# First attention: its last four heads as straight code without look-ahead, the last sum's store and the x load in other places

## The chip, the cores and the metric

One core of a Trainium2 chip runs the whole program in one launch. The metric is the device time in microseconds of that launch, median of several runs. The engines named below are TensorE (PE), VectorE (DVE), ScalarE (ACT), GpSimd (POOL) and SyncE (SP), whose instruction stream issues nearly all DMAs.

## The reference, cut to what matters

```python
x = x + L0_xattn(layernorm(x), ctx_512, ...)   # latent cross attention, 8 batches x 16 heads
x = x + L0_ffn(layernorm(x), ...)              # feed-forward on 64 chosen rows of each sequence
x = x + L1_xattn(layernorm(x), ctx_512, ...)
x = x + L1_ffn(layernorm(x), ...)              # mixture of experts
```

In the first attention, for each of 8 batches and 16 heads: queries of 256 positions are projected to 192 numbers (`q_big`), turned by their rotary table, projected into the 64-number space of the context rows; scores against 1601 context rows, softmax, and a weighted sum of the rows (`ctx_c`, 256 x 64). An output projection follows:

```python
scores = einsum('bhsr,bhlr->bhsl', q_r, k_r)
attn = softmax(scores)
ctx_c = einsum('bhsl,bld->bhsd', attn, kv_r)
ctx = einsum('bhsd,hkd->bhsk', ctx_c, w_kc_kv) ... ; return ctx @ Wo.T
```

## The kernel before, in words

The program is a row of stages, each a block in which every engine has its own instruction stream; at the end of a block all engines meet. The change lies at the end of `phase_attention0` and at the start of `phase_project0_ffn0`, which follows it.

**The attention stage** works on `N` = 128 heads (8 batches x 16). Head n is pipelined over the engines, with orders written out by hand. The main part is a loop of 32 turns on each of PE, ACT, DVE and POOL, four heads (`AHEAD`) a turn; the body is the same for every head apart from odd and even ones. For head n, PE's body (L927 and on) runs:

- `scores` (L826): the rest of the scores of head n and most of those of head n+1. 26 matmuls of 256 columns a head, in four groups g of key tiles (4, 4, 4 and 1 tiles). 22 of the 26 in a body belong to head n+1.
- `values` (L844, L847): the weighted sum of head n, 26 pairs of matmuls, 129 and 65 columns, one with the probabilities' high parts (`prob`), one with their low parts (`rest`). They add into the PSUM tile `c_psV`.
- `maxima` (L810): eight matmuls of 400 or 401 columns for head n+2, whose row maxima DVE takes (`reduce_max`, L1132) and joins (`join`).
- `shift` (L814): one transposition of these maxima for head n+1.
- the queries of later heads, made for a pair p of heads at a time: `q_first` (L764, 12 matmuls) in odd bodies and `q_second` (L764, 6) in even ones, `q_lat_high` (L790, 6) and `q_lat_low` (L796, 3) in odd ones, all of 256 columns. DVE, ACT and POOL turn and split them (`turn_first`, `turn_second`, `rope_high`, `rope_low` L1251, `q_high`, `q_low`).

ACT takes the exponential of each score group (`exp`, L1011) and, when all of head n's values are summed, drains `c_psV` (L1077). POOL makes the low parts (`rest_of`, L1243: three large ones and a small one per head; it takes the probabilities minus their rounded high part), and in `total` (L1257, L1259) adds the two halves of the drained tile of head n-1 and keeps the softmax sum in `rec`. A `rest_of` of group g waits for that group's exponential; `values` of group g wait for that `rest_of`; the exponential of group g of the next head waits for those `values`, as there is one buffer per group.

So the look-ahead of the last turn belongs to heads 128 and 129, which don't exist: the loop computes them from the first batch's data, which SP loads once more for it (`batch_steps(B - 1, 0)`, with `last=following` the refills of keys and values).

SP stores each head's sum to DRAM (`acc_scr`, L715), the last after the loops (L744), and then waits until everything it issued has landed. DVE, after its loop, inverts the first batch's sums of softmax and scales that batch's rows (`scale_heads`, L518, two multiplications of 1024 columns). The end of the block follows.

**The next stage** projects and normalizes batch by batch. For batch b, DVE scales the rows of batch b+1 (`scale_batch`, L518), adds the projection to x (`add_rows`, L1507), takes statistics, logits and the choice of rows; PE transposes the scaled rows (`turn`, L1624) and projects them (`project`, L1633). PE's projection of batch b+1 waits until the addition of batch b has emptied its PSUM tile. Before the first scaling DVE waits for five small constant loads, and before the first addition for the whole of x:

```python
            sp.dma_start(x[:], t["x"]...).then_inc(in_x, 16)          # L1454, 2 MB
            ... five small loads: br, wr, upper, iota, base           # L1455 to L1459
            for b in range(2, B):
                sp.wait_ge(t_full, 4 * (b - 2) + 4)
                load_heads(sp, t, keep, b)                            # L511, 2 x 512 KB
            ...
            dve.wait_ge(in_c, 80)                                     # the five
            for b in range(B):
                if b + 1 < B:
                    scale_batch(dve, nc.vector, b + 1)
                add_rows(b)                                           # b == 0: waits in_x
```

Of the kernel before, what the change touches and what calls it, by code (L numbers as in the profile page):

```python
# [522 lines left out]
def phase_attention0(nc, ctx, t, keep):  # L523
# [102 lines left out]
    with nc.Block() as block:  # L626
        @block.sync
        def _(sp):
# [94 lines left out]
            def batch_steps(b, following):  # L723
# [18 lines left out]
            batch_steps(B - 1, 0)  # L742
            sp.wait_ge(summed, 2 * N + 2)
            sp.dma_start(t["acc_scr"][N], acc[1][:, :, DC:2 * DC]).then_inc(sent[1], 16)  # L744
            for u in range(2):
                sp.wait_ge(sent[u], 16 + 16 * (N // 2))
            sp.wait_ge(in_wA, 16 * (N // 2 + 4))
            sp.wait_ge(in_wR, 16 * (N // 2 + 3))
            for g in range(4):
                sp.wait_ge(in_kk[g], 32 * (B + 1))  # L750
                sp.wait_ge(in_v[g], 16 * (B + 1))
            for c in range(len(CHUNKS)):
                sp.wait_ge(in_kkm[c], 16 * (B + 1))
            sp.wait_ge(in_xb, 32 * (B + 1))
            sp.wait_ge(in_m, 16 * (N // 2 + 3))

        @block.tensor
        def _(pe):
# [168 lines left out]
            with pe.Fori(0, N // AHEAD) as j:  # L927
                for u in range(AHEAD):
# [41 lines left out]
                    maxima(n + 2, p2, 7, s2)  # L970

        @block.scalar
        def _(act):
# [29 lines left out]
            def exp(n, g, slot):  # L1003
                lo, hi = GROUPS[g]
                r = P if hi < LT else LLAST
                w = (hi - lo) * S
                act.wait_ge(s_full, 4 * n + g + 1)

                act.wait_ge(in_kk[(g + 2) % 4], 32 * ((n + (g + 2) // 4) // H0) + 32)
# [47 lines left out]
            with act.Fori(0, N // AHEAD) as j:  # L1057
                for u in range(AHEAD):
# [20 lines left out]
                    if u % 2 == 0:  # L1079
                        rope_high(p, slice(2, 3), ropedR)  # L1080

        @block.vector
        def _(dve):
# [42 lines left out]
            def reduce_max(n, k):  # L1126
                c, st = divmod(k, ST)
                dve.wait_ge(mx_full, PASSES * n + k + 1)
                if st == 0:
# [72 lines left out]
            with dve.Fori(0, N // AHEAD) as j:  # L1202
                for u in range(AHEAD):
# [22 lines left out]
                    reduce_max(n + 2, 7)  # L1226
            dve.wait_ge(summed, 2 * H0 + 2)
# [3 lines left out]
            dve.wait_ge(keep["in_acc"][0], 32)  # L1231
            for s in range(ST):
                scale_heads(nc.vector, keep, 0, s)

        @block.gpsimd
        def _(pool):
# [17 lines left out]
            def total(n, i):  # L1254

                pool.wait_ge(pv_drained, n + 1)
                nc.gpsimd.tensor_tensor(acc[i][:, :, DC:2 * DC], acc[i][:, :, DC:2 * DC], acc[i][:, :, 0:DC],  # L1257
                                        ALU.add).then_inc(summed, 1)
# [15 lines left out]
            with pool.Fori(0, N // AHEAD) as j:  # L1274
# [11 lines left out]
            total(N, 1)  # L1286
# [102 lines left out]
def phase_project0_ffn0(nc, ctx, t, keep, ahead, x, xn):  # L1389
# [1446 lines left out]
def build(nc, t):  # L2836
    LIVE.clear()
    with ExitStack() as whole:
        def sb(ctx, name, shape, dt=F32):
# [21 lines left out]
            "rec": rec,  # L2861
            "in_acc": [new_semaphore(nc, f"in_acc{i}") for i in range(2)],
# [109 lines left out]
```

## Time and profile before

| | us |
|---|---|
| median of 3 runs | 1640.25 (1639.94 to 1640.4) |
| the profiled execution's own time | 1644.53 |
| its span, first to last instruction | 1642.9 |
| PE busy in the span | 1567.9 |
| DVE busy | 1308.3 |
| POOL busy | 1153.0 |
| ACT busy | 1062.5 |

The loop of the attention stage ends near 1145 us of the span; the next stage's first instructions stand at 1148.3 us. The span is read stage by stage: in each, the engine that is never idle, or the wait that ends last, sets the length. In a timeline a row's first number is its start from the span's beginning, the second its length; matmuls are pipelined, so two that follow each other without a gap are told apart by their starts. The brackets give the idle time before a row and what ended it.

### The profile page before, as it was taken

How to read it: one execution, taken by the hardware profiler on the slowest of the kernel's cores; microseconds unless marked ns; L12 is line 12 of the kernel's file. 1: busy time of each engine (PE TensorE's matmuls, PEld its weight loads, DVE VectorE, ACT ScalarE, POOL GpSimd, SP SyncE). 2: the span in 40 equal slices, each digit the busy share in tenths (PEclk: the TensorE clock that was granted, in tenths of full speed). 3: DMA queues.
4: the chain of work that ended last, by engine and by line, in shares of the span. 5: the costliest groups of instructions: out<-in, count | busy, mean ns of one | idle time of the engine just before them, and what ended most of it. 6: DMA issues, size and time to landing. Idle time of an engine off the chain costs nothing. (4 is left out here: it accounts for less than half of the span.)

```text
span 1642.9 us, 50082 instructions
## 1 busy us (share of the span) xinstructions
PE 1567.9 (95%) x16337; PEld 1280.1 (78%) x16337; DVE 1308.3 (80%) x3062; ACT 1062.5 (65%) x2174; POOL 1153.0 (70%) x1102
## 2 busy tenths in 40 slices
PE   5879999999999999999999999999999899999998
PEld 4658888888888888888888888887886445556787
DVE  6888888888898888888898888888783578885223
ACT  5877777777777777777777777776322466664121
POOL 5439999999999999999999999998100214431321
PEclk8699999999999999999999999999999999999999
DMA  9731121121122122112112115312840011101344
GB/s 259 237 89 49 48 81 49 49 76 49 48 64 65 40 66 72 42 57 74 48 46 83 40 56 127 76 54 76 212 86 1 15 35 65 66 8 54 101 149 161
DMA packets 184952, 126.23 MB, mean 77 GB/s; under 512 B 107578, under 2 KB 172008, under 8 KB 184512
## 3 DMA queue, kind: packets, MB, share of 16 engines
q1 hardware_dynamic: 183360, 121.53, 26.4%
q0 software_dynamic: 1536, 3.99, 0.7%
q8 instruction: 31, 0.51, 0.1%
q14 instruction: 25, 0.20, 0.0%
HBM read 82.24 MB, written 24.48 MB: 65 GB/s over the span
## 5 line engine op out<-in xcount | busy, mean ns | idle before, releaser
L1243 POOL TENSOR_TENSOR c_rest<-c_prob 128x1024 f16<-128x1024 f32 (+1 forms) x513 | 817.1, 1608 | 37.8 <-ACT c_prob L1011 16.7
L1132 DVE TENSOR_REDUCE c_mxp<-c_psM 128x1 f32<-128x400 f32 (+1 forms) x1040 | 578.1, 571 | 56.8 <-PE c_psM L810 37.1
L1011 ACT ACTIVATE c_prob<-c_psS,ln,c_exp_scale 128x1024 f32<-128x1024 f32 (+1 forms) x514 | 528.3, 1040 | 145.1 <-PE c_psS L826 141.8
L826 PE MATMUL c_psS<-c_q,c_kk 128*128 128x256 f16 (+1 forms) x3350 | 513.0, 273 | 0.5 <-DVE c_ropeA L1091 0.4
L844 PE MATMUL c_psV<-c_vb,c_prob 128*128 128x129 f16 (+1 forms) x3328 | 420.5, 221 | 1.1 <-ACT c_acc L1077 1.1
L847 PE MATMUL c_psV<-c_vb,c_rest 128*128 128x65 f16 (+1 forms) x3328 | 394.5, 193 | 0.0
L826 PEld LDWEIGHTS c_psS<-c_q,c_kk 128*128 128x128 f16 (+1 forms) x3350 | 311.0, 99 | 66.2 <-issue 1.0
L810 PE MATMUL c_psM<-c_kkm,c_q 128*128 128x400 f16 (+1 forms) x1040 | 347.0, 334 | 3.5 <-DVE c_mxp L1132 2.9
L847 PEld LDWEIGHTS c_psV<-c_vb,c_rest 128*128 128x128 f16 (+1 forms) x3328 | 303.0, 98 | 28.7
L844 PEld LDWEIGHTS c_psV<-c_vb,c_prob 128*128 128x128 bf16 (+1 forms) x3328 | 312.7, 98 | 14.0 <-ACT c_acc L1077 1.4
L2221 ACT ACTIVATE g_prob<-g_psS,g_bias 128x128 f32<-128x128 f32 (+1 forms) x256 | 103.8, 426 | 49.8 <-DVE g_bias L2271 49.8
L1251 POOL TENSOR_TENSOR c_ropedL<-c_roped,c_ropedH 128x512 f16<-128x512 f32 (+1 forms) x132 | 118.4, 915 | 21.7 <-ACT c_ropedH L979 14.7
L810 PEld LDWEIGHTS c_psM<-c_kkm,c_q 128*128 128x128 f16 x1040 | 101.1, 97 | 10.0 <-DVE c_mxp L1132 4.2
L979 ACT ACTIVATE c_ropedH<-c_roped 128x512 f16<-128x512 f32 (+1 forms) x132 | 68.9, 522 | 48.5 <-DVE c_roped L1097 48.2
L764 PE MATMUL c_psS<-c_xb,c_w2s 128*128 128x256 f16 x768 | 94.3, 273 | 0.0
L1323 POOL TENSOR_SCALAR xn_rows<-x_rows,f_n_agg,f_n_rstd 128x256 f32<-128x256 f32 x3 | 3.9, 1316 | 128.5 <-DVEq L1340 128.5
L2676 DVE TENSOR_TENSOR m_g<-m_s,m_psH 128x256 f32<-128x256 f32 (+1 forms) x48 | 20.0, 419 | 78.6 <-ACT m_s L2623 66.8
L764 PEld LDWEIGHTS c_psS<-c_xb,c_w2s 128*128 128x128 f16 x768 | 73.3, 98 | 9.8
L986 ACT ACTIVATE c_q<-c_psQ 64x256 f16<-64x256 f32 x132 | 49.8, 377 | 47.5 <-PE c_psQ L796 46.0
L999 ACT ACTIVATE c_q<-c_psM 32x128 f16<-32x128 f16 x258 | 68.8, 267 | 9.4 <-PE c_psM L814 3.2
L1087 DVE TENSOR_TENSOR c_ropeB<-c_psS,c_tabB 128x256 f32<-128x256 f32 x128 | 48.4, 420 | 33.2 <-PE c_psS L764 33.2
L2623 ACT ACTIVATE m_s<-m_psH 128x256 f32<-128x256 f32 (+1 forms) x48 | 18.2, 382 | 80.8 <-PE m_psH L2500 69.6
(336 smaller groups left out, 2491.3 us busy)
## 6 DMA issues: line engine op xcount, KB each, us to landing
c_w2s<-w_scr SPq DMA_DIRECT2D x67, 256.0 KB, 2.6
c_ms<-m_scr SPq DMA_DIRECT2D x67, 192.0 KB, 2.7
c_w2s<-w_scr SPq DMA_DIRECT2D x66, 128.0 KB, 2.0
acc_scr<-c_acc SPq DMA_DIRECT2D x129, 64.0 KB, 2.0
kv<-acc_scr SPq DMA_DIRECT2D x16, 512.0 KB, 6.3
m_w<-in_L_ffn_W SPq DMA_DIRECT2D x16, 352.0 KB, 3.5
c_vb<-V SPq DMA_DIRECT2D x27, 129.0 KB, 2.0
c_kk<-KK SPq DMA_DIRECT2D x27, 128.0 KB, 2.0
```

What stands on the lines that cost most here:

```text
L764: mm = pe.matmul(out, weights[:, w, c], xb[:, x, c, :], start=(c == 0 and i == 0), stop=(c == DK - 1 and i == 2))
L810: pe.matmul(psM[:, st, 0:w], q1[slot][:, st * P:(st + 1) * P], kkm[:, c0:c0 + w], start=True, stop=True).then_inc(mx_full, 1)
L826: mm = pe.matmul(psS[g % 2][0:r, i * S:(i + 1) * S], src[:, (lo + i) * P:(lo + i) * P + r], mov[slot][:, :], start=(one == 0 and i % 2 == ...
L844: pe.matmul(psV[:, st * W:(st + 1) * W], high[0:r, c0:c0 + P], vb[0:r, i, :], start=(i == 0 and st == 0), stop=False, skip_group_check=True)
L847: mm = pe.matmul(psV[:, st * W + DC:(st + 1) * W], rest[g][0:r, c0:c0 + P], vb[0:r, i, DC:W], start=False, stop=(i == LT - 1), skip_group_ ...
L979: nc.scalar.activation(ropedH[:, blocks, :], roped[:, blocks, :], ACT.Copy).then_inc(rh_done, 1)
L999: last = nc.scalar.activation(q2[slot][0:2 * SHIFT_ROWS, st * P:(st + 1) * P], shiftT[st * 2 * SHIFT_ROWS:(st + 1) * 2 * SHIFT_ROWS, :], A ...
L1011: nc.scalar.activation(prob[g][0:r, 0:w], psS[g % 2][0:r, 0:w], ACT.Exp, bias=keep["ln1024"][0:r, :], scale=exp_scale[slot][0:r, :]).then_ ...
L1132: nc.vector.tensor_reduce(mxp[:, st, c:c + 1], psM[:, st, 0:CHUNKS[c][1]], AX.X, ALU.max).then_inc(mx_done, 1)
L1243: nc.gpsimd.tensor_tensor(rest[g][0:r, 0:w], prob[g][0:r, 0:w], high[0:r, 0:w], ALU.subtract).then_inc(rest_done, 1)
L1251: nc.gpsimd.tensor_tensor(ropedL[:, blocks, :], roped[:, blocks, :], ropedH[:, blocks, :], ALU.subtract).then_inc(rl_done, 1)
L2221: ins = nc.scalar.activation(prob[k % 2][:, i * w:(i + 1) * w], psS[k % 2][:, i * w:(i + 1) * w], ACT.Exp, bias=bias[k % 2][:, i:i + 1], a ...
```

## The change

PE, ACT, DVE and POOL run 31 turns of their loops instead of 32, and the last four heads (124 to 127) are written out after them. In that code:

- PE has no query matmuls (`q_first`, `q_second`, `q_lat_high`, `q_lat_low`), no scores and no transposition for head 128, no maxima for heads 128 and 129. The order of the rest is as before but for small moves; where the maxima of a further head stood ahead of scores, head 126's body waits for ACT's `shift_copy` itself.
- ACT has no `rope_high`, `q_high`, `q_other`, and no exponentials for head 128.
- DVE has no turns and `q_low`, and no maxima beyond head 127. After its loop it inverts the first batch's sums as before, and then waits for POOL's last low part (`rest_done` of 4 N) before it scales.
- POOL has no `rope_low` and no low part of head 128. The last `total` writes to a place inside the large tile `kv` (`last_acc`) that outlives the stage.
- SP has no query loads and no refills for these four heads; it stores the sums of heads 123 to 126, and not the last one.

The next stage's SP stream begins with the store of that last sum, then the five small constant loads, then x; the load of batch 7's heads, which reads that sum, waits for the store.

```diff
-                four(H0 // AHEAD - 1, last=following)
+                if not ends:
+                    four(H0 // AHEAD - 1, last=following)
...
-            batch_steps(B - 1, 0)
-            sp.wait_ge(summed, 2 * N + 2)
-            sp.dma_start(t["acc_scr"][N], acc[1][:, :, DC:2 * DC]).then_inc(sent[1], 16)
+            batch_steps(B - 1, 0, ends=True)
+            for n in range(N - AHEAD, N):
+                sp.wait_ge(summed, 2 * n + 2)
+                sp.dma_start(t["acc_scr"][n], acc[(n + 1) % 2][:, :, DC:2 * DC]).then_inc(sent[(n + 1) % 2], 16)
...
-            with pe.Fori(0, N // AHEAD) as j:
+            with pe.Fori(0, N // AHEAD - 1) as j:
...
+            for u in range(AHEAD):
+                n, s1, s2 = N - AHEAD + u, (u + 1) % AHEAD, (u + 2) % AHEAD
+                scores(n, 2, u, (6, 8))
+                scores(n, 3, u)
+                values(n, 0, (0, 1))
+                if n + 2 < N:
+                    maxima(n + 2, (n + 2) // 2, 0, s2)
+                values(n, 0, (1, 4))
+                if n + 1 < N:
+                    scores(n + 1, 0, s1, (0, 4))
+                    pe.wait_ge(mcol_done, 2 * n + 4)
+                    shift(n + 1)
+                values(n, 1, (0, 2))
+                if n + 2 < N:
+                    maxima(n + 2, (n + 2) // 2, 1, s2)
+                elif n + 1 < N:
+                    pe.wait_ge(shift_done, n + 2)
...
+                values(n, 3)
+                if n + 1 < N:
+                    scores(n + 1, 2, s1, (0, 6))
+                if n + 2 < N:
+                    maxima(n + 2, (n + 2) // 2, 7, s2)
...
+            for u in range(AHEAD):
+                n = N - AHEAD + u
+                exp(n, 2, u)
+                if n + 1 < N and u % 2 == 0:
+                    shift_copy(n + 1, (u + 1) % AHEAD)
+                exp(n, 3, u)
+                if n + 1 < N and u % 2 == 1:
+                    shift_copy(n + 1, (u + 1) % AHEAD)
+                if n + 1 < N:
+                    exp(n + 1, 0, (u + 1) % AHEAD)
+                    exp(n + 1, 1, (u + 1) % AHEAD)
+                act.wait_ge(pv_done, 4 * n + 8)
...
+            for u in range(AHEAD - 1):
+                n = N - AHEAD + u
+                join(n + 1)
+                if n + 2 < N:
+                    for k in range(PASSES):
+                        if k == PASSES - 1:
+                            scale_of(n + 2, (u + 2) % AHEAD)
+                        reduce_max(n + 2, k)
             dve.wait_ge(summed, 2 * H0 + 2)
...
             dve.wait_ge(keep["in_acc"][0], 32)
+            dve.wait_ge(rest_done, 4 * N)
             for s in range(ST):
                 scale_heads(nc.vector, keep, 0, s)
...
-            total(N, 1)
+            for n in range(N - AHEAD, N):
+                rest_of(n, 1)
+                rest_of(n, 2)
+                rest_of(n, 3)
+                total(n, (n + 1) % 2)
+                if n + 1 < N:
+                    rest_of(n + 1, 0)
+            total(N, 1, keep["last_acc"])
...
-            sp.dma_start(x[:], t["x"].rearrange("b (s p) d -> p (b s) d", p=P)).then_inc(in_x, 16)
+            sp.dma_start(t["acc_scr"][B * H0], keep["last_acc"]).then_inc(keep["last_sent"], 16)
             sp.dma_start(br[:], t["L0_ffn_b_r"].partition_broadcast(P)).then_inc(in_c, 16)
...
             sp.dma_start(base[:], t["cap_base"]).then_inc(in_c, 16)
+            sp.dma_start(x[:], t["x"].rearrange("b (s p) d -> p (b s) d", p=P)).then_inc(in_x, 16)
             for b in range(2, B):
                 sp.wait_ge(t_full, 4 * (b - 2) + 4)
+                if b == B - 1:
+                    sp.wait_ge(keep["last_sent"], 16)
                 load_heads(sp, t, keep, b)
```

## Rows read from the trace of the kernel before

**Rows 1.** The span, from the view of cores.

```profile
core 0: 1642.9 us, clock 0.980
```

**Rows 2.** Windows: length, PE, PE load, DVE, ACT, POOL, clock, DMA share.

```profile
1113.20:1129.30 16.10, 16.10 (x204) 13.94 (x201) 14.32 (x35) 12.20 (x21) 15.74 (x15) 1.00 0.22 64
1145.90:1162.00 16.10, 11.77 (x57) 10.11 (x58) 6.66 (x10) 3.16 (x6) 7.82 (x2) 0.89 0.82 217
1280.00:1300.00 20.00, 17.29 (x92) 9.63 (x89) 12.42 (x38) 13.45 (x26) 8.34 (x6) 1.00 0.00 0
```

**Rows 3.** Timeline of POOL at the end of the attention: start, us, line, operation.

```profile
1112.41 4.42 POOL L1243 TENSOR_TENSOR c_rest<-c_prob 128x1024 f16<-128x1024 f32 x3 [0.21 <-ACT c_prob L1011]
...
1117.50 2.25 POOL L1243 TENSOR_TENSOR c_rest<-c_prob 128x1024 f16<-128x1024 f32 x1
1119.72 1.78 POOL L1251 TENSOR_TENSOR c_ropedL<-c_roped,c_ropedH 128x512 f16<-128x512 f32 x2
...
1137.50 4.31 POOL L1243 TENSOR_TENSOR c_rest<-c_prob 128x1024 f16<-128x1024 f32 x3
...
1144.68 0.45 POOL L1257 TENSOR_TENSOR c_acc<-c_acc 128x128 f32<-128x128 f32 x1 [0.22 <-ACT c_acc L1077]
```

**Rows 4.** Timeline of PE there: start, us (pipelined), line, count.

```profile
1143.42 0.33 PE L810 MATMUL c_psM<-c_kkm,c_q 128*128 128x401 f16 x1
1143.59 0.22 PE L844 MATMUL c_psV<-c_vb,c_prob 65*128 65x129 f16 x1
...
1143.68 0.22 PE L844 MATMUL c_psV<-c_vb,c_prob 65*128 65x129 f16 x1
...
1143.77 0.82 PE L826 MATMUL c_psS<-c_q,c_kk 128*128 128x256 f16 x6
1144.42 0.33 PE L810 MATMUL c_psM<-c_kkm,c_q 128*128 128x401 f16 x1
1148.49 0.30 PE L1624 MATMUL e_ps<-kv 128*128 128x128 f32 x1 [3.74 <-PEq L626]
```

**Rows 5.** Timeline of ACT there, the last drain.

```profile
1144.22 0.38 ACT L1077 ACTIVATE c_acc<-c_psV 128x258 f32<-128x258 f32 x1
```

**Rows 6.** Timeline of DVE: one turn addition, then the stage boundary.

```profile
1117.32 0.68 DVE L1097 TENSOR_TENSOR c_roped<-c_ropeA,c_ropeB 128x512 f32<-128x512 f32 x1
...
1145.66 2.36 DVE L518 TENSOR_TENSOR kv<-kv 128x1024 f32<-128x1024 f32 x2
...
1159.43 2.36 DVE L518 TENSOR_TENSOR kv<-kv 128x1024 f32<-128x1024 f32 x2 [9.09 <-DMA e_base<-in_cap_base]
1161.71 0.74 DVE L1507 TENSOR_TENSOR x_rows<-x_rows,e_ps 128x256 f32<-128x256 f32 x2
...
1168.24 1.23 DVE L518 TENSOR_TENSOR kv<-kv 128x1024 f32<-128x1024 f32 x1
```

**Rows 7.** Timeline of the DMA queue of SP (its issues) at the boundary.

```profile
1145.45 0.60 SPq L744 DMA_DIRECT2D acc_scr<-c_acc  x1
1148.31 0.39 SPq L1454 DMA_DIRECT2D x_rows<-in_x  x1
...
1152.12 0.47 SPq L1459 DMA_DIRECT2D e_base<-in_cap_base  x1
1152.65 5.94 SPq L511 DMA_DIRECT2D kv<-acc_scr  x2
```

**Rows 8.** DMA issues of the boundary: count, KB, us from issue to landing.

```profile
x_rows<-in_x SPq DMA_DIRECT2D x1, 2048.0 KB, 9.7
...
e_upper<-in_upper SPq DMA_DIRECT2D x1, 32.0 KB, 6.0
...
e_base<-in_cap_base SPq DMA_DIRECT2D x1, 8.0 KB, 7.1
...
kv<-acc_scr SPq DMA_DIRECT2D x1, 512.0 KB, 8.2
...
acc_scr<-c_acc SPq DMA_DIRECT2D x3, 64.0 KB, 2.0
```

More of the change, by code:

```diff
@@ L721, in step, with batch_steps @@
                     refill_values(sp, last, 3)
-            def batch_steps(b, following):
+            def batch_steps(b, following, ends=False):
                 def four(j, last=None, x=None):
@@ L970, in _ @@
                     maxima(n + 2, p2, 7, s2)
+            for u in range(AHEAD):
[16 more added lines that the diff above has]
+                if n + 1 < N:
+                    scores(n + 1, 0, s1, (4, 8))
+                if n + 2 < N:
+                    maxima(n + 2, (n + 2) // 2, 2, s2)
+                values(n, 1, (2, 4))
+                if n + 2 < N:
+                    maxima(n + 2, (n + 2) // 2, 3, s2)
+                if n + 1 < N:
+                    scores(n + 1, 1, s1, (0, 2))
+                values(n, 2, (0, 1))
+                if n + 2 < N:
+                    maxima(n + 2, (n + 2) // 2, 4, s2)
+                if n + 1 < N:
+                    scores(n + 1, 1, s1, (2, 6))
+                if n + 2 < N:
+                    maxima(n + 2, (n + 2) // 2, 5, s2)
+                if n + 1 < N:
+                    scores(n + 1, 1, s1, (6, 8))
+                values(n, 2, (1, 4))
+                if n + 2 < N:
+                    maxima(n + 2, (n + 2) // 2, 6, s2)
+                values(n, 3)
+                if n + 1 < N:
+                    scores(n + 1, 2, s1, (0, 6))
+                if n + 2 < N:
+                    maxima(n + 2, (n + 2) // 2, 7, s2)
         @block.scalar
@@ L1007, in exp @@
                 act.wait_ge(s_full, 4 * n + g + 1)
-                act.wait_ge(in_kk[(g + 2) % 4], 32 * ((n + (g + 2) // 4) // H0) + 32)
+                if not (isinstance(n, int) and n + (g + 2) // 4 == N):
+                    act.wait_ge(in_kk[(g + 2) % 4], 32 * ((n + (g + 2) // 4) // H0) + 32)
                 act.wait_ge(pv_done, 4 * n + g + 1)
@@ L1056, in _ @@
             q_other(1, 2)
-            with act.Fori(0, N // AHEAD) as j:
+            with act.Fori(0, N // AHEAD - 1) as j:
                 for u in range(AHEAD):
@@ L1128, in reduce_max @@
                 dve.wait_ge(mx_full, PASSES * n + k + 1)
-                if st == 0:
+                if st == 0 and not (isinstance(n, int) and n + (c + 1) // len(CHUNKS) == N):
                     dve.wait_ge(in_kkm[(c + 1) % len(CHUNKS)],
@@ L1201, in _ @@
             q_low(1, 2)
-            with dve.Fori(0, N // AHEAD) as j:
+            with dve.Fori(0, N // AHEAD - 1) as j:
                 for u in range(AHEAD):
@@ L1252, in rope_low, with total @@
                                         ALU.subtract).then_inc(rl_done, 1)
-            def total(n, i):
+            def total(n, i, out=None):
                 pool.wait_ge(pv_drained, n + 1)
-                nc.gpsimd.tensor_tensor(acc[i][:, :, DC:2 * DC], acc[i][:, :, DC:2 * DC], acc[i][:, :, 0:DC],
-                                        ALU.add).then_inc(summed, 1)
+                nc.gpsimd.tensor_tensor(acc[i][:, :, DC:2 * DC] if out is None else out, acc[i][:, :, DC:2 * DC],
+                                        acc[i][:, :, 0:DC], ALU.add).then_inc(summed, 1)
                 nc.gpsimd.tensor_copy(keep["rec"][:, bass.ds(n, 1), :].rearrange("p o s -> p (o s)"),
@@ L1273, in _ @@
             pool.wait_ge(v_low, B)
-            with pool.Fori(0, N // AHEAD) as j:
+            with pool.Fori(0, N // AHEAD - 1) as j:
                 for u in range(AHEAD):
@@ L2861, in build @@
             "rec": rec,
+            "last_acc": kv[:, B * LT * DC - n_rec + ST - ST * DC:B * LT * DC - n_rec + ST].rearrange(
+                "p (s d) -> p s d", s=ST),
+            "last_sent": new_semaphore(nc, "last_sent"),
             "in_acc": [new_semaphore(nc, f"in_acc{i}") for i in range(2)],
```

19 lines of the change are left out of this document (10 added, 9 removed).

## The prediction

> **What bounds the kernel now.** First the cores: one core, a span of 1642.9 us [rows 1]. The profiled execution took 1644.53 us, the median of the runs is 1640.25; I take the sum against the span of 1642.9 and carry the difference over to the median unchanged. The change touches only the last four heads of the first attention and the entry of the next stage, so everything before about 1112.4 us of the span, and everything after about 1168 us, should keep its length and only move. The windows say who is full: in a pair of heads, 16.10 us, PE is busy for all 16.10, POOL for 15.74 and DVE for 14.32 [rows 2]. PE sets the pace and POOL stands 0.4 us behind it. So work taken from PE alone is worth little; what is taken from POOL counts. The timelines of POOL, PE, ACT and DVE then show the end: POOL finishes the low parts of head 127 at 1137.50 + 4.31 = 1141.81 [rows 3]; PE still has work up to 1144.4, and the drain waits for it at 1144.22 [rows 4, 5]; the next stage issues its first DMA at 1148.31 [rows 7]. There DVE stands still for 9.09 us until the constant `e_base` lands [rows 6].
>
> **1. What PE loses.** In-order starts give a price each: six score matmuls from 1143.77 to 1144.42, 0.109 us each; a maxima matmul 0.17 (1143.42 to 1143.59); a values pair 0.09 (1143.59 to 1143.68) [rows 4]. Removed are 24 + 12 + 18 query matmuls and 22 scores, 76 x 0.109 = 8.3 us, and 16 maxima, 2.7 us, together 11.0 (the one transposition is below 0.1). Four heads, two windows of 16.1 less a little, take 32.1 us of PE; 21.0 or so remain [rows 2].
>
> **2. What the four heads then cost: POOL.** POOL begins head 124's low parts at 1112.41 and ends head 127's at 1141.81, 29.40 us. Of that only the two pairs of `rope_low`, 1.78 us each, are useless: 3.56 [rows 3]. 25.84 us remain, above PE's 21.0, so POOL becomes the bound and the last low part ends at 1138.25. The removed low part of head 128 came after it and belongs to step 3. From below: beside DVE's turn addition of 0.68 us the low part takes 2.25 us, 0.36 more than the 1.89 that it takes otherwise (4.42 for two large and a small one leaves about that) [rows 3, 6]; with the turns gone two such excesses go, 0.7 us at most. From above: POOL waited 0.21 us for an exponential before head 124 [rows 3]; if it does so two times a head now that nothing separates its parts, that is 4 x 0.4 = 1.6 us less the 0.7 that is idle already (twice 16.10 - 15.74 [rows 2]), 0.9. I take 0, between the two.
>
> **3. From the last low part to the next stage.** Now 6.50 us pass from 1141.81 to 1148.31: head 128's low part, the total at 1144.68, the store of 0.60 us at 1145.45 that lands 2.0 us later, and DVE's scaling, 1145.66 + 2.36 = 1148.02, which ends last; 0.29 us more to the first issue [rows 3, 6 to 8]. Afterwards DVE waits for the last low part, scales in 2.36, and the stage ends 0.29 later: 2.65. Beside it lie two to eight values pairs of head 127 (0.7 us at 0.09 [rows 4]), the drain of 0.38 [rows 5] and the total of 0.45 and its small copy, 1.8 us in all with the handovers: hidden under the scaling by 0.6. But that total runs beside a DVE multiplication that reads two tensors of SBUF, and the low part above paid 0.36 for such a neighbour [rows 3, 6]. Cost 0 if hidden, 0.65 if the total can only start when the scaling is over; I take 0.25, nearer to the row. The inversion of the sums (DVE has been idle) and the store cost nothing here; with cover gone they would be 0.34 and 2.0. So 6.50 becomes 2.90: 3.60 gained. The Trainium skill (SBUF — State Buffer, Terms, "shared port pair") says that the loser of that port fully blocks and doesn't share bandwidth; by it the 0.65 would be paid and the sum be 0.4 worse. The low part's excess of 0.36 beside 0.68 neither proves nor denies it, as their starts differ (1117.50 against 1117.32).
>
> The stage's end thus moves from 1148.31 to 1141.15, by 3.56 + 3.60 = 7.16 us.
>
> **4. The entry of the next stage.** Call its start S. Now `add_rows(0)` starts at S + 13.40 (1161.71): the constants land at 1152.12 + 7.1 = S + 10.9, and the scaling of batch 1, 2.36 us, comes after them; x has landed at S + 9.7 and is not waited for [rows 6 to 8]. Afterwards SP issues the store (0.60 where x took 0.39) and the constants, the last at S + 4.0. With no 2 MB in front they land in about the 2.0 us of a store [rows 8], S + 6, and batch 1 is scaled by S + 8.5 while PE is busy with batch 0. x is issued at S + 4.34 + 0.21 = S + 4.55 [rows 7]. Its landing took 9.7 us with 232 KB of constants among its 2048; scaled by 2048/2280 it is 8.7. I take the middle, 9.2: x lands at S + 13.75 and the addition starts at S + 13.85, 0.45 later than now. Bounds: 8.7 us gives S + 13.35, nothing; the case with batch 2's loads between is a rival. So the 9.09 us stall isn't gained: the wait for constants is replaced by one for x, since x now starts 4.2 us later. The Trainium skill (DMA: Bandwidth & Descriptors, Queues, rings and completion order) has each DMA engine take descriptors in ring order; by it loads issued behind x can't hold it up, and x would land with the 32 KB load behind it, `e_upper`, at 1151.16 + 6.0 or 8.9 us after its issue, 0.3 better than my sum. The row has it at 9.7, later than that small load, so the order of landings isn't that of the issues [rows 8].
>
> Batch 2's rows: their first load landed at 1152.65 + 8.2, 7.4 us before DVE scales them at 1168.24; the second was held in the queue until 1158.59, 9.6 us before [rows 6 to 8]. All that traffic now starts 4.2 us after S later, so some 3 us of slack stay: 0. The removed refills and query loads had nobody behind them but the end: 0. The new wait on `last_sent` stands before batch 7's load, six batches after a store of 2 us: 0.
>
> **Sum:** -3.56 - 3.60 + 0.45 = -6.7 us; span 1636.2, median 1640.25 - 6.7 = 1633.5 us.
>
> **The rivals.** (a) x comes later still: batch 2's two loads of 512 KB are issued right behind it (now 4.3 us after it [rows 7]) and share the engines with it. If one of them gets ahead it costs 9.2 x 512/2048 = 2.3 us, both 4.6: 1635.8 to 1638.1 us. For it speaks that landings overtake each other; against it that x moved ahead of everything now. (b) The four heads don't shorten: PE waits for low parts, ACT for PE, POOL for exponentials in a ring, and step 2 gives nothing: 1637.0. For it: single buffers per group, so each part hands over to the next; against: PE has 4.8 us to spare over four heads. (c) Slower: PE has gaps in the four heads, 21.0 of 25.84 us busy, 81%, and the granted clock falls to its lower level (1.2 instead of 2.4 GHz). If it fell for all of it, PE would need 42.0 us, 16.2 more than POOL: 1649.7. It decides once 4.8 us of its work run at half, and the result is slower than before when 11.5 us do. Against it: at 17.29 of 20.00 us busy the clock was 1.00; for it: around PE's idle 3.74 us the mean was 0.89 [rows 2, 4]. (d) The change doesn't do what it says, as something else holds the stage's end: that would be seen as (b) with step 3 gone too, 1640.7.
>
> **How the numbers follow.** The forecast 0.62, with its own range 1631.1 (rests shorter by 0.7, no port cost, x 0.45 earlier, the idle 0.7 gone, and the 0.3 by which runs differ: 2.4 in all) to 1635.8; (a) 0.18; (b) 0.13; (c) 0.04; (d) 0.03. The range is 1631.1 to 1638.1, to the end of (a); (c) and (d) stay out. 0.2%, about what a measurement of this kernel can tell from no change, is 3.3 us: faster means under 1637.0. That takes in the forecast, two thirds of (a) and half of (b): 0.81; within 0.2%: 0.15; slower: 0.04.
>
> **What would show it.** In the changed profile: POOL's last L1243 ends about 25.8 us after head 124's first one (rival b: 29.4), PE has gaps before `values` and POOL none; DVE's L518 follows within 0.1 us; the first SP issue of the next stage comes 2.9 us after the last low part; DVE's stall in front of L1507 names x_rows, with L518 of batch 1 near S + 6; from there to the end the distances are those of before. The prediction is wrong if L1507 starts before S + 12.5 or after S + 15, if the clock leaves 1.00 within the four heads, or if a stage after 1168 us changes its length by over 1 us.

## The result, and the profile after

The changed kernel takes 1630.49 us (median of 4 runs, 1630.03 to 1631.92); the kernel before, run beside it, 1640.1 us (1638.79 to 1640.4). The ratio is 0.9944, with a 95% interval of 0.9933 to 0.9956: about 9 us faster, where 6.7 were forecast. 1630.5 lies 0.6 us below the low end of the range. The profiled execution took 1630.33 us.

The span, from the view of cores:

```profile
core 0: 1628.5 us, clock 0.983
```

POOL's timeline of the last four heads (the page's columns: start, us, line, operation, idle time before it and what ended it), to be laid beside [rows 3]:

```profile
1109.44 6.37 POOL L1308 TENSOR_TENSOR c_rest<-c_prob 128x1024 f16<-128x1024 f32 x4
...
1116.69 1.89 POOL L1308 TENSOR_TENSOR c_rest<-c_prob 128x1024 f16<-128x1024 f32 x1 [0.34 <-ACT c_prob L1052]
1118.77 4.38 POOL L1308 TENSOR_TENSOR c_rest<-c_prob 128x1024 f16<-128x1024 f32 x3 [0.18 <-ACT c_prob L1052]
...
1124.07 1.89 POOL L1308 TENSOR_TENSOR c_rest<-c_prob 128x1024 f16<-128x1024 f32 x1 [0.38 <-ACT c_prob L1052]
...
1131.29 6.17 POOL L1308 TENSOR_TENSOR c_rest<-c_prob 128x1024 f16<-128x1024 f32 x4 [0.17 <-ACT c_prob L1052]
1137.41 0.46 POOL L1322 TENSOR_TENSOR c_acc<-c_acc 128x128 f32<-128x128 f32 x1
1137.81 1.18 POOL L1324 COPY kv<-c_acc 128x2 f32<-128x2 f32 x1
1138.95 0.45 POOL L1322 TENSOR_TENSOR kv<-c_acc 128x128 f32<-128x128 f32 x1
1139.35 1.18 POOL L1324 COPY kv<-c_acc 128x2 f32<-128x2 f32 x1
```

Head 124's first low part starts at 1109.44 and head 127's last ends at 1131.29 + 6.17 = 1137.46: 28.02 us. Before, it was 31.50: the 29.40 us of the prediction begin at 1112.41, with head 124's second low part, and the first, which stands 2.10 us ahead of it at 1110.31, belongs to the stretch:

```profile
1110.31 1.89 POOL L1243 TENSOR_TENSOR c_rest<-c_prob 128x1024 f16<-128x1024 f32 x1
```

POOL's waits for an exponential are short, 0.17 to 0.38 us, and there are five of them.

The same stretch as a window (length, PE, PE load, DVE, ACT, POOL, clock, DMA share, GB/s):

```profile
1109.44:1137.46 28.02, 24.33 (x331) 20.61 (x329) 13.21 (x33) 18.63 (x27) 26.63 (x23) 1.00 0.05 11
```

POOL is busy for 26.63 of 28.02 us, PE for 24.33, and the granted clock is 1.00, the upper of its two levels. In the kernel before, the same stretch has POOL busy for 30.60 of 31.50 us and PE for all 31.50:

```profile
1110.31:1141.81 31.50, 31.50 (x399) 27.38 (x396) 28.02 (x68) 23.83 (x40) 30.60 (x27) 1.00 0.27 82
```

DVE at the boundary, beside [rows 6]:

```profile
1137.59 2.90 DVE L518 TENSOR_TENSOR kv<-kv 128x1024 f32<-128x1024 f32 x2 [9.53 <-POOL c_rest L1308]
...
1146.21 2.36 DVE L518 TENSOR_TENSOR kv<-kv 128x1024 f32<-128x1024 f32 x2 [2.79 <-DMA e_base<-in_cap_base]
1153.65 0.75 DVE L1582 TENSOR_TENSOR x_rows<-x_rows,e_ps 128x256 f32<-128x256 f32 x2 [5.08 <-DMA x_rows<-in_x]
...
1159.71 1.23 DVE L518 TENSOR_TENSOR kv<-kv 128x1024 f32<-128x1024 f32 x1
```

The scaling of the first batch follows the last low part by 0.13 us, takes 2.90 instead of 2.36, and has ended by 1140.49, but the next stage starts only at 1141.39. What it starts on is in SP's queue (beside [rows 7]) and in the waits of SP (line waited for: total, times, longest):

```profile
1139.02 0.53 SPq L746 DMA_DIRECT2D acc_scr<-c_acc  x1
1141.39 0.34 SPq L1526 DMA_DIRECT2D acc_scr<-kv  x1
1141.78 0.43 SPq L1527 DMA_DIRECT2D e_br<-in_L_ffn_b_r  x1
...
1143.68 0.43 SPq L1531 DMA_DIRECT2D e_base<-in_cap_base  x1
1144.15 0.43 SPq L1532 DMA_DIRECT2D x_rows<-in_x  x1
1144.98 8.32 SPq L511 DMA_DIRECT2D kv<-acc_scr  x2
```

```profile
SPq L626 <- DMA acc_scr<-c_acc: 1.2, 1, 1.2
```

The store of head 126's sum is issued at 1139.02, when POOL's copy (1137.81 + 1.18) is through, and SP waits at the end of the block until it has landed. Call the first issue of the next stage S again (1141.39). The x load is issued at S + 2.76 and lands 9.5 us later (beside [rows 8]):

```profile
x_rows<-in_x SPq DMA_DIRECT2D x1, 2048.0 KB, 9.5
```

### The profile page after: what moved, and what is told of

Its sections match the earlier page's. It is cut to its first block and busy times, and to the rows that moved or that the text cites. A ratio compares the mean times of both kernels' runs of the same rounds, so it can differ in the third digit from the quotient of the medians.

```text
span 1628.5 us, 49586 instructions
## 1 busy us (share of the span) xinstructions
PE 1555.9 (96%) x16244; PEld 1269.8 (78%) x16244; DVE 1291.7 (79%) x3021; ACT 1055.8 (65%) x2158; POOL 1150.2 (71%) x1097
## 5 line engine op out<-in xcount | busy, mean ns | idle before, releaser
L1188 DVE TENSOR_REDUCE c_mxp<-c_psM 128x1 f32<-128x400 f32 (+1 forms) x1024 | 569.5, 572 | 59.4 <-PE c_psM L807 40.2
L807 PE MATMUL c_psM<-c_kkm,c_q 128*128 128x400 f16 (+1 forms) x1024 | 341.7, 334 | 4.1 <-DVE c_mxp L1188 2.9
L1316 POOL TENSOR_TENSOR c_ropedL<-c_roped,c_ropedH 128x512 f16<-128x512 f32 (+1 forms) x128 | 114.8, 916 | 21.7 <-ACT c_ropedH L1019 14.7
L2353 DVE COPY g_pT<-g_psT 128x1024 f32<-128x1024 f32 x48 | 58.7, 1224 | 14.0 <-PE g_psT L2199 12.9
```

What stands on the lines that cost most here:

```text
L807: pe.matmul(psM[:, st, 0:w], q1[slot][:, st * P:(st + 1) * P], kkm[:, c0:c0 + w], start=True, stop=True).then_inc(mx_full, 1)
L1188: nc.vector.tensor_reduce(mxp[:, st, c:c + 1], psM[:, st, 0:CHUNKS[c][1]], AX.X, ALU.max).then_inc(mx_done, 1)
L1316: nc.gpsimd.tensor_tensor(ropedL[:, blocks, :], roped[:, blocks, :], ropedH[:, blocks, :], ALU.subtract).then_inc(rl_done, 1)
```

## The experiments

Twelve kernels were run, in three groups, each group on one chip with the kernel before beside it (medians of before: 1646.21, 1639.67 and 1647.54 us). Between chips only ratios are compared. One table holds the steps, all read from timelines as above. R3 is the end of the last low part; "chain" is the time from head 124's first low part to the scaling of batch 2 in the next stage, the first point after which every kernel does the same at the same distances, up to the entry of the second attention (below). In the kernels whose next stage doesn't begin with the store (before, before_again, x_moved_alone, last_store_in_stage), S is its first issue all the same. Every experiment has one trace, the kernels before and after have two each; between the two of one kernel, the chain differs by 0.25 to 0.28 us.

| kernel | start to R3 | R3 to S | S to `add_rows(0)` | S to batch 2 | chain | ratio of the run, 95% interval |
|---|---|---|---|---|---|---|
| before | 31.50 | 6.50 | 13.40 | 19.93 | 57.93 | |
| before_again | 31.50 | 6.50 | 13.68 | 20.21 | 58.21 | 0.9999 (0.9989 to 1.0008) |
| after | 28.02 | 3.93 | 12.26 | 18.32 | 50.27 | 0.9944 (0.9933 to 0.9956) |
| after_again | 28.00 | 3.94 | 12.03 | 18.08 | 50.02 | 0.9944 (0.993 to 0.9958) |
| x_first | 28.02 | 3.93 | 13.15 | 19.68 | 51.63 | 0.9955 (0.9942 to 0.9969) |
| x_moved_alone | 31.5 | 6.49 | 11.77 | 18.02 | 56.0 | 0.9988 (0.9979 to 0.9997) |
| no_low_wait | 29.71 | 2.94 | 11.95 | 18.01 | 50.66 | 0.9944 (0.9931 to 0.9958) |
| early_total_half_scale | 28.56 | 2.13 | 12.17 | 18.23 | 48.92 | 0.9943 (0.9929 to 0.9956) |
| last_store_in_stage | 28.0 | 5.52 | 11.49 | 18.82 | 52.35 | 0.9957 (0.9945 to 0.9969) |
| last_head_low_on_dve | 26.52 | 3.07 | 12.45 | 18.51 | 48.10 | 0.9931 (0.9917 to 0.9945) |
| all_together | 26.51 | 2.08 | 12.24 | 18.29 | 46.88 | 0.9934 (0.992 to 0.9948) |
| pe_keeps_useless | 30.61 | 3.93 | 12.04 | 18.56 | 53.10 | 0.9962 (0.9947 to 0.9977) |
| x_split | 28.01 | 3.93 | 7.40 | 18.01 | 49.95 | 0.995 (0.9938 to 0.9963) |
| low_on_dve_x_split | 26.52 | 3.07 | 8.63 | 19.28 | 48.87 | 0.9939 (0.9927 to 0.9951) |

**Where x is loaded.** The theory of the prediction says that x's later issue costs 0.45 us; the result says that it is a gain. Two kernels ask this from both sides. x_first is the changed kernel with x ahead of the constants; x_moved_alone is the kernel before with x behind them and nothing else changed.

```diff
+            sp.dma_start(x[:], t["x"]...).then_inc(in_x, 16)
             sp.dma_start(br[:], ...)
...
-            sp.dma_start(x[:], t["x"]...).then_inc(in_x, 16)
```

> The changed kernel with one edit undone: in the next stage's SP stream x (2 MB) is loaded ahead of the five constants again, behind the last sum's store. Theory (the constants' issues and landings are slow behind x): the DVE stall in front of the scaling of batch 1 is back, near 9 us, that scaling starts about 11 us after the stage's first issue S instead of 4.8, the first addition at S + 13.4 instead of S + 12.3, and PE's spread of batch 0 follows later, so 1.1 to 1.6 us more than the changed kernel's 1630.5: 1631.6 to 1632.1. Rival (x's landing alone decides, as the prediction had it, 0.45 in favour of x first): 1630.0.

> The kernel before with one part of the change alone: x is loaded behind the five constants; tail and store as before. Theory: the same 1.1 to 1.6 us as between the changed kernel and x_first, so about 1638.7 against 1640.1. The prediction's own step 4: 0.45 slower, 1640.5. If the last sum's store ahead of the constants is what matters: no change.

SP's queue in x_first and then in x_moved_alone:

```profile
1143.37 0.43 SPq L1527 DMA_DIRECT2D x_rows<-in_x  x1
1143.85 2.10 SPq L1528 DMA_DIRECT2D e_br<-in_L_ffn_b_r  x1
1145.98 0.43 SPq L1529 DMA_DIRECT2D e_wr<-in_L_ffn_W_r  x1
```

```profile
1148.65 0.34 SPq L1454 DMA_DIRECT2D e_br<-in_L_ffn_b_r  x1
1149.04 0.43 SPq L1455 DMA_DIRECT2D e_wr<-in_L_ffn_W_r  x1
...
1150.95 0.42 SPq L1459 DMA_DIRECT2D x_rows<-in_x  x1
```

Behind the 2 MB load one constant's issue takes 2.10 us (in before_again two take 1.28 and 1.16), ahead of it 0.34 to 0.43. So x ahead costs SP 1.5 to 1.7 us of issuing, and the constants are slow to land; x behind waits for 2.3 us of issues only. The move gives the kernel before 1.9 to 2.2 us on the chain (ratio 0.9988, 2.0 us, by its interval 0.5 to 3.5), and undoing it takes 1.4 to 1.6 from the changed kernel (by the ratios, 0.9955 against 0.9944, it can't be told from nothing), whose DVE row then reads:

```profile
1153.86 2.36 DVE L518 TENSOR_TENSOR kv<-kv 128x1024 f32<-128x1024 f32 x2 [8.84 <-DMA e_base<-in_cap_base]
```

The old stall of about 9 us is back. A rival for a part of the loss is the clock: from S to batch 2's scaling its mean is 0.84 in x_first, with PE busy for 19.29 of 19.68 us, and 0.91 in the changed kernel, with 17.75 of 18.32. But `add_rows(0)` follows DVE's scaling without a gap in x_first, and at that point 0.9 to 1.1 of the 1.4 to 1.6 us are there already. Only the rest, behind it, can be the clock's.

**Is x then the next thing to shorten?** x_split loads batch 0's part of x ahead of the constants and the rest behind them.

```diff
+            sp.dma_start(x[:, 0:ST], t["x"][0:1]...).then_inc(in_x, 16)
             sp.dma_start(br[:], ...)
...
-            sp.dma_start(x[:], t["x"]...).then_inc(in_x, 16)
+            sp.dma_start(x[:, ST:NT], t["x"][1:B]...).then_inc(in_xr, 16)
```

> The changed kernel with the load of x in two: batch 0's 256 KB behind the last sum's store and ahead of the constants, the other seven batches where x is now. Theory: DVE's wait of 5 us for x goes, but PE is busy with batch 0's projections and batch 1's transpositions until S + 12.4 and spreads batch 0's logits only after the projection that follows, so the third scaling comes 0.3 to 0.5 us earlier: 0.4 us faster, and the wait moves from x to PE. Rival (x's wait is worth its length): 2 us or more faster.

```profile
1149.29 0.41 DVE L1585 TENSOR_TENSOR x_rows<-x_rows,e_ps 128x256 f32<-128x256 f32 x1
1152.63 0.42 DVE L1585 TENSOR_TENSOR x_rows<-x_rows,e_ps 128x256 f32<-128x256 f32 x1 [2.93 <-PE e_ps L1711]
```

The first addition comes 4.9 us earlier, at S + 7.40, without a wait for x; its second half then waits for PE, and batch 2's scaling starts only 0.3 us earlier than in the changed kernel (0.1 against after_again). The wait for x of 5.08 us in DVE's rows is hidden but for that, and the ratios agree (0.995 against 0.9944). What it hid behind is PE, which in the 12 us behind S is busy for 11.81 at a clock of 0.86 in the changed kernel already. The same 12 us in the two kernels with x split, first x_split, then low_on_dve_x_split:

```profile
1141.89:1153.89 12.00, 11.81 (x62) 10.91 (x63) 5.92 (x14) 3.57 (x6) 7.82 (x2) 0.86 0.82 233
```

```profile
1141.93:1153.93 12.00, 11.72 (x50) 10.56 (x51) 4.75 (x8) 2.75 (x4) 7.81 (x2) 0.75 0.86 236
```

PE is full in both, at a mean granted clock of 0.86 and 0.75, and where it is 0.75 batch 2's scaling comes at S + 19.28 instead of 18.01.

**What holds the end of the attention.** The prediction put DVE's scaling last. The rival is SP's wait for the store of head 126's sum. early_total_half_scale makes POOL take that total ahead of head 127's low parts, and leaves half of the scaling to the next stage; last_store_in_stage puts the last sum's store back into the attention; no_low_wait drops DVE's wait for the last low part.

```diff
+                if n == N - 1:
+                    total(n, (n + 1) % 2)
                 rest_of(n, 1)
...
-            for s in range(ST):
-                scale_heads(nc.vector, keep, 0, s)
+            scale_heads(nc.vector, keep, 0, 0)
...
+            scale_heads(nc.vector, keep, 0, 1)
```

> The changed kernel with two moves at its end: POOL's total of head 126 comes ahead of head 127's second low part instead of behind its last one, and DVE scales only the first half of batch 0 before the stage's end and the second half first thing in the next stage. Theory (the store of head 126's sum, issued 1.6 us after the last low part and landed 2.0 us later, ends the stage): the last low part 0.6 later, but only the last total (1.85 us) and 0.3 behind it, so the next stage starts 2.5 to 2.8 us after the last low part instead of 3.9: 0.6 to 0.8 us faster, 1629.8, and SP waits for no landing at the end. Rival (the end is held by DVE's scaling or by a fixed barrier of 0.9 us behind it): the gap between the last work and the first issue stays 0.9.

```diff
+            sp.wait_ge(summed, 2 * N + 2)
+            sp.dma_start(t["acc_scr"][N], acc[1][:, :, DC:2 * DC]).then_inc(sent[1], 16)
...
-            total(N, 1, keep["last_acc"])
+            total(N, 1)
...
-            sp.dma_start(t["acc_scr"][B * H0], keep["last_acc"])...
```

> The changed kernel with one part undone: the last head's sum is stored by the attention stage again, after its total, and SP waits for it there; the next stage's stream begins with the constants. Theory: the last total ends 3.1 us after the last low part (its copy held by DVE's scaling), the store lands 2.0 us later and the next stage starts 0.37 after that, 5.4 us after the last low part instead of 3.9; SP then reaches x 0.4 earlier. Net 1.1 us slower than the changed kernel. Rival (the store was hidden under something else): no change, as with the prediction's step 3, which put DVE's scaling at the end.

```diff
-            dve.wait_ge(rest_done, 4 * N)
```

> The changed kernel without DVE's wait for the last low part: DVE scales the first batch as soon as its own work is done, about 9 us earlier, beside POOL's low parts. The result is the same. Theory of an exclusive port: each of the two multiplications holds POOL for up to 1.2 us, the last low part comes up to 2.4 us later, and the end after it shrinks from 3.9 to about 3.0 us, since the copy of 1.18 us is 0.18 again and the store follows earlier: net 1 to 1.5 us slower, 1631.5 to 1632. Rival, the port is shared at half the cost: 0.3 slower, 1630.8. Rival, no contention: the end alone shrinks, 1629.6.

POOL at the end of no_low_wait and, below, its DVE row:

```profile
1128.39 5.36 POOL L1307 TENSOR_TENSOR c_rest<-c_prob 128x1024 f16<-128x1024 f32 x3 [0.19 <-ACT c_prob L1052]
1133.72 1.43 POOL L1321 TENSOR_TENSOR c_acc<-c_acc 128x128 f32<-128x128 f32 x1
...
1141.36 0.45 POOL L1321 TENSOR_TENSOR c_acc<-c_acc 128x128 f32<-128x128 f32 x1
1141.76 0.18 POOL L1323 COPY kv<-c_acc 128x2 f32<-128x2 f32 x1
```

```profile
1130.33 4.50 DVE L518 TENSOR_TENSOR kv<-kv 128x1024 f32<-128x1024 f32 x2
```

In no_low_wait the scaling is over long before the end, and the stage still ends 2.94 us after R3: total 0.40 to its successor, copy 0.18, store 2.0, and some 0.4 to the first issue. In the changed kernel the copy takes 1.18, and 3.93 us pass: 0.99 more, the copy's excess of 1.00. With the store of head 126 out of the way (early_total_half_scale, whose last total follows the drain at R3 + 1.04), 2.13 us are left: the last copy, again of 0.18 us, ends 0.34 us before S, and head 126's store has landed some 4 us before S. (This kernel moves the total and half of the scaling at once, and which of the two gives how much isn't shown.) With the last store back in the stage it is 5.52, the store's issue at 1142.69 following a second copy of 1.18; so moving that store is worth 1.6 us at the end. On the chain it is 2.1, where 1.1 were expected; the other 0.5 lie behind S, where the clock's mean is 0.86 instead of 0.91 and PE is busy for 18.58 of 18.82 us, and it isn't shown that the store's place brings them. The chain of the end is thus total, copy, store, landing in the changed kernel, in no_low_wait and in last_store_in_stage (there with the last head's store), and DVE's scaling decides through the 1.00 us by which it delays the copy.

no_low_wait also prices the wait itself: started early, the scaling runs beside low parts, three of which take 5.36 instead of 4.42 us and a total 1.43 instead of 0.46. Start to R3 grows by 1.7 us, the end shrinks by 1.0, and the chain is 0.4 to 0.6 longer than in the changed kernel, where 1 to 1.5 were expected. The ratios, 0.9944 both, can't tell that apart. DVE pays as much as POOL here: its two multiplications take 4.50 us instead of 2.36, the second alone 2.95.

**What bounds the four heads.** pe_keeps_useless adds 48 matmuls of 256 columns on PE's last four bodies, twelve in each, some 5.2 us, that nobody reads. last_head_low_on_dve gives head 127's low parts to DVE.

```diff
                 scores(n, 3, u)
...
+                q_rows(psQ[:, 0:S], wR)
+                q_rows(psQ[:, 0:S], wR)
```

> The changed kernel with useless work put back on PE alone: 12 query matmuls of 256 columns in each of the last four bodies, 48 x 0.109 = 5.2 us, into a PSUM tile that nobody reads. Theory (POOL bounds the written-out heads): PE goes from 21.0 to 26.2 us in 28.0, so most of it fits its gaps: head 124's first low part to the last one from 28.0 to at most 29.2 us. Rival (the ring through PE, ACT and POOL bounds them, each handover in series): all 5.2 us are added, 33.2 us.

```diff
             for n in range(N - AHEAD, N):
-                rest_of(n, 1)
-                rest_of(n, 2)
-                rest_of(n, 3)
+                if n < N - 1:
+                    rest_of(n, 1)
+                    rest_of(n, 2)
+                    rest_of(n, 3)
...
+            for g in range(len(GROUPS)):
+                nc.vector.tensor_tensor(rest[g]..., prob[g]..., high..., ALU.subtract).then_inc(rest_done, 1)
             dve.wait_ge(rest_done, 4 * N)
```

> The changed kernel with head 127's four low parts made by DVE, which stands idle there, instead of POOL. Theory (POOL's low parts bound the written-out heads): they end 1.3 to 1.8 us earlier, as DVE takes about 1.2 us for a large one where POOL takes 1.9 and the exponentials are there early; the last low part then follows the last exponential by about 1.5 us. End and entry as in the changed kernel: 1.3 to 1.8 us faster. Rival (the ring through PE and ACT bounds them): the last low part stays where it is, no change.

The added 5.2 us of PE cost 2.6 (28.0 to 30.61), and POOL's longest wait for an exponential grew from 0.4 to 1.3 us. Neither theory had that. PE was idle for 3.7 us (24.33 of 28.02 busy), so at least 1.5 of the 5.2 had no room, and PE is now busy for 28.77 of 30.61 us, POOL for 26.59. That the other 1.1 us are lost because every low part, exponential and `values` hands over to the next in one buffer is argued and not shown. Taking four of POOL's sixteen low parts away gives 1.5 us of the 6.2 that they take, as DVE then does them in 4.2:

```profile
1132.90 2.49 DVE L1303 TENSOR_TENSOR c_rest<-c_prob 128x1024 f16<-128x1024 f32 x2 [3.38 <-ACT c_prob L1052]
1135.74 1.68 DVE L1303 TENSOR_TENSOR c_rest<-c_prob 128x1024 f16<-128x1024 f32 x2 [0.35 <-ACT c_prob L1052]
1137.45 2.66 DVE L518 TENSOR_TENSOR kv<-kv 128x1024 f32<-128x1024 f32 x2
```

Its end is shorter too, 3.07 instead of 3.93: POOL, freed of head 127's low parts, takes head 126's total at 1134.42, and the store behind it, issued at 1135.86, lands 3.0 us later, 1.6 us before S. That is one more sign that this store held the end.

**All at once, and both kernels again.** all_together is last_head_low_on_dve with half of the scaling moved to the next stage; low_on_dve_x_split joins last_head_low_on_dve to x_split; before_again and after_again are the two kernels unchanged.

> The low parts of head 127 on DVE, POOL's total of head 126 as early as it can be, and the second half of batch 0 scaled in the next stage. Theory: both gains add, since one shortens the heads and the other the end behind them: head 124's first low part to the third scaling of the next stage 47.3 to 47.8 us where the changed kernel has 50.3, early_total_half_scale 48.9, so 2.5 to 3 us faster than the changed kernel. Rival: with the low parts gone from POOL the exponentials bound head 127, and the second gain is only half there: 1.5 us.

> Two gains in one kernel: head 127's low parts on DVE (1.9 us between head 124's first low part and the third scaling of the next stage in its own trace) and x in two loads (0.4 expected): 47.7 us for that distance where the changed kernel has 50.0 to 50.3. If the clock at the entry of the second attention stays at its upper level, the median is 2.3 us below the changed kernel's; if it doesn't, 0.7.

> The kernel before, word for word, once more, for its trace beside those of the others on one chip. If the time outside the edited stages is noise, its distances up to the attention and behind the next stage's entry lie anywhere within what the other traces show, among them one stall of PE of 3.9 us in the last stage (L2510) that the first trace of the kernel before had and that of the changed kernel had not; if the change moved them, it shows the stall again and the changed kernel again none.

> The changed kernel, word for word, once more. From its first trace, measured between head 124's first low part and the third scaling of the next stage: 50.3 us where before has 57.9, 7.7 us less. If that is the whole effect, the medians differ by about 7.7 us; if the stall of 3.9 us in the last stage is gone for good as well, by 11.6. The first four runs gave 9.6.

The pair gave 1639.98 and 1630.86 us, spans of 1638.4 and 1627.8. Of these 10.6 us, 8.2 lie in the chain, 1.3 between batch 2's scaling and ACT's first `kT` drain (it copies the first keys of the second attention out of PSUM), and 1.0 before the chain, in code that is the same (there the fourteen traces start their chains anywhere from 1109.4 to 1112.3 us, in no order of kernels). The 1.3 us point to a place that the change doesn't touch, the entry of the second attention, 125 to 127 us behind S. Here it is as PE rows and as a window from PE's first matmul behind an idle time of 2.7 us to that drain, of before_again and then of after_again:

```profile
1277.86 1.01 PE L1837 MATMUL f_psA<-kv,f_wq 128*128 128x128 f32 x4
1278.80 5.52 PE L1848 MATMUL f_psA<-f_cT,f_wkvT 64*128 64x512 f32 x16
```

```profile
1276.53:1280.91 4.38, 4.38 (x22) 3.02 (x24) 4.38 (x14) 2.17 (x5) 0.00 (x0) 0.66 0.02 4
```

```profile
1268.68 0.60 PE L1912 MATMUL f_psA<-kv,f_wq 128*128 128x128 f32 x4
1269.21 2.04 PE L1923 MATMUL f_psA<-f_cT,f_wkvT 64*128 64x512 f32 x8
```

```profile
1267.34:1270.37 3.03, 3.03 (x22) 2.25 (x24) 3.03 (x10) 2.07 (x4) 0.00 (x0) 1.00 0.00 0
```

The same 22 matmuls take 4.38 us in one and 3.03 in the other. In before_again the clock goes to its lower level (1.2 GHz) for a part of them, and in after_again it stays at the upper one. Up to PE's first of these matmuls the distance from batch 2's scaling is 106.9 to 107.0 us in all kernels (107.4 in the three with low parts on DVE), so the whole difference lies in these few microseconds. Up to the drain it takes 111.3 to 111.5 us in before and before_again, and 109.9 to 110.0 in after, after_again, x_first, x_moved_alone, no_low_wait, last_store_in_stage, pe_keeps_useless and x_split, with last_head_low_on_dve at 110.4. In three experiments the clock fell as in before: early_total_half_scale takes 111.5, and all_together and low_on_dve_x_split, whose windows follow, 112.05 and 113.1:

```profile
1265.83:1270.49 4.66, 4.66 (x22) 3.36 (x24) 4.66 (x15) 2.28 (x4) 0.00 (x0) 0.63 0.01 2
```

```profile
1268.59:1274.27 5.68, 5.68 (x22) 4.32 (x24) 5.65 (x21) 2.39 (x4) 0.00 (x0) 0.50 0.01 1
```

This would explain why early_total_half_scale and all_together gained 1.35 and 1.2 us on the chain (against after and last_head_low_on_dve) and showed nothing in the median: in their traces the entry took 1.5 to 1.6 us back. Which shift of the stages puts the entry at which level wasn't found. Before and after had the same level in both of their traces each, but whether the level goes with the kernel or with the execution isn't shown: the traced execution of low_on_dve_x_split was the slowest of six, 1639.23 us where the others took 1635.78 to 1637.87. That kernel was expected at 47.7 us on the chain and has 48.87, with PE at the lower clock behind S; its ratio, 0.9939 against 0.9944, puts it 0.8 us below the changed kernel, within the intervals.

x_moved_alone shows how far a trace can be read. Its chain is 1.9 to 2.2 us shorter than before's and its entry 1.4 to 1.6, together more than 3, while the medians give 2.0.

Fastest of all are last_head_low_on_dve (1629.28 us) and all_together (1629.70) against 1630.86 for after_again on the same chip. The intervals of their ratios overlap, so a gain of 1 to 1.5 us over the changed kernel is likely and not shown. On the chain the two gains of all_together add: 46.88 us, a little below the 47.3 to 47.8 expected.

## Why the prediction was off

**Step 2 held.** The four heads lost 3.48 us (31.50 to 28.02) where 3.56 were forecast, though the 25.8 and 29.4 us given as marks left out head 124's first part. POOL, 26.63 of 28.02 us busy, sets their length far more than PE with 24.33. That the total came so near is in part luck, since two small terms in it cancel. POOL's busy time fell by 3.97 us, 0.4 more than the 3.56, as low parts that took 2.25 beside DVE's turns take 1.89 (the bound from below), and its idle time grew by 0.5, from 0.90 to 1.39, with the waits of 0.17 to 0.38 us for exponentials (the bound from above). Step 1 was rougher: "PE has 4.8 us to spare" was too generous, 3.7 were left, and pe_keeps_useless shows that PE is near to bounding the stretch too. Rival (b) is refuted, and so is (c): the clock stayed at 1.00 in the four heads. Rival (a) didn't come either: batch 2's loads were issued 0.8 us behind x, and x landed after 9.5 us.

**Step 3 was mis-sized.** 6.50 became 3.93, not 2.90: 2.57 gained instead of 3.60. Its term "the total and its small copy hidden under the scaling" failed, in a way that the sum didn't hold: the copy of head 126's total was priced at nothing, but it goes ahead of a store whose landing the stage waits for. The step had named 2.0 us for a store with its cover gone, for the last one; it was the last but one whose cover went. By the Trainium skill (SBUF — State Buffer, Terms, "shared port pair") the engine that loses the port is blocked and doesn't share, and here the trace agrees: a copy of 0.18 us takes 1.18 beside a scaling, and in x_first the total 1.44 instead of 0.45. By that rule's 0.65 the step would have given 3.30, which is nearer and still 0.63 short, since what was late was a store behind the blocked copy. DVE's scaling, at 2.90 instead of 2.36 us, would have ended the stage at 3.3 by itself, so 0.4 of the 1.0 us is a slower scaling and 0.6 the store. Rival (d) had the right form, something else holds the stage's end, but not the size: most of the step's gain stayed.

**Step 4 had the wrong sign; this is the step that failed.** "0.45 later" was 1.14 earlier at `add_rows(0)`, and 1.61 at batch 2's scaling (1.65 and 2.13 in the second pair). x's landing was right, 9.5 us for 9.2. Wrong was "x is issued at S + 4.55": it is at S + 2.76. The range had a bound for x's landing and none for its issue, and `add_rows(0)` at S + 12.26 lies below the S + 12.5 that the prediction had named as a sign that it is wrong. I took the issue times of the five constants from the trace of before, where they stood behind the 2 MB load, and that position is what the change removes. Each took 0.43 us with x behind them. The last half microsecond comes from behind `add_rows(0)`, 6.53 us to batch 2's scaling before and 6.06 after. So the sum of the chain is -3.48 - 2.57 - 1.61 = -7.66 us where it was -6.7: an error of 1.0 us in one direction in step 3 and of 2.1 us in the other in step 4, so the total looks better than its parts.

**The rest.** 9.1 to 9.6 us were measured in the medians; the chain holds 7.7 to 8.2 of them and the entry of the second attention 1.3 to 1.5. "Everything after 1168 us should keep its length" thus failed too, by more than the 1 us that the prediction named as its limit. Without that entry, which is the clock's doing, the time would have been near 1632 and within the range. The two first traces differ by more, 14.4 us: 0.9 of it lie before the four heads and 3.9 are one PE stall in the last stage (below), which kernels of both kinds show. The rest, some 0.4 us, isn't accounted for.

## What to carry to other kernels

A duration read in a trace belongs to the order in which it was issued: when a change moves a large transfer, the issue times of what stood behind it are no price for what will stand ahead. When the work at a stage's end is shortened, list every store whose landing the block waits for, and price the tiny instruction in front of each of them beside its new neighbour. A local gain of about 1 us can be swallowed or doubled by the clock at an entry 120 us later, as the traces here suggest, so read the gain at the changed place first and in the median second.

## What the runs showed of the hardware

- A POOL copy of 128 x 2 numbers takes 0.18 us alone and 1.18 beside a DVE multiplication of 128 x 1024 that reads two SBUF tensors (1.23 us each). DVE loses 0.54 there: its two multiplications take 2.90 instead of 2.36. Beside two low parts and a total (no_low_wait) DVE's two take 4.50, and POOL loses 0.94 and 0.98 us on the same stretch, so neither engine is always the one that waits. A total of 0.45 takes 1.28 beside a low part on DVE (last_head_low_on_dve).
- A load's issue on SP takes 0.34 to 0.43 us, and 1.2 to 2.1 us right behind a 2 MB load. The constants behind x landed 6 to 8 us after their issue ([rows 8] has two of them); ahead of it the last one, issued at 1143.68, had landed by 1146.21, 2.5 us.
- At an entry after 2.7 to 3.2 us of PE idling, the same 22 matmuls took 3.03 us at a granted clock of 1.00, 4.38 to 4.66 at 0.63 to 0.66 and 5.68 at 0.50, in kernels that are the same from there on.
- In the last stage PE stood still once for 3.9 to 4.0 us with nothing that the profile names, in the first trace of before and in six experiments; x_split has 6.8 us there, and last_store_in_stage 3.2 us at the same matmul, put down to DVE. These eight experiments are all those of the two groups whose kernel before took 1646 and 1648 us, and none of the four of the group with 1640 has it, nor has after. Kernels of both kinds are on either side (x_moved_alone with it, before_again without), so it isn't the change; whether it goes with the chip or with the execution, and what causes it, stays open.
